# Four attention and feed-forward stages on one core: loads moved ahead, input normalised inside local attention, token shift started early, value projections of latent attention split

## The reference

```python
def _layer(x, wqkv, qs, ksc, wo, lg, lb, w1, b1, w2, b2):
    h = shift_token(x)                      # half of the features from the row before
    q, k, v = split(h @ wqkv)               # 8 heads of 64
    q, k = rotary_xpos(l2norm(q) * qs, l2norm(k) * ksc)
    x = x + local_attention(q, k, v) @ wo
    h = layernorm(shift_token(x)) * lg + lb
    a, g = split(h @ w1 + b1)
    return x + (a * gelu(g)) @ w2 + b2
```

## Time and profile before

| | us |
|---|---|
| median of 3 runs (4442.75 to 4448.69) | 4447.3 |
| the profiled execution | 4451.65 |
| its span, first to last instruction | 4449.6 |
| TensorE busy | 3951.2 |
| VectorE busy | 3057.0 |
| ScalarE busy | 2683.5 |
| GpSimd busy | 1837.7 |

### The profile page before, as it was taken

One profiled execution on the slowest core, in us unless ns is written; L12 is line 12 of the kernel. 1 busy time (PEld: TensorE's weight loads), 2 busy tenths in 40 slices (PEclk: granted clock), 3 DMA queues, 4 the chain that ended last, 5 costly groups with the idle time before them and its releaser, 6 DMA issues. The chain is left out here.

```text
span 4449.6 us, 104983 instructions
## 1 busy us (share of the span) xinstructions
PE 3951.2 (89%) x35227; PEld 3054.4 (69%) x35481; DVE 3057.0 (69%) x7210; ACT 2683.5 (60%) x6345; POOL 1837.7 (41%) x1769
## 2 busy tenths in 40 slices
PE   5999999938999988899999788999999999989999
PEld 4777777726666665566666546777767776669998
DVE  5888888867888865688888574555555555546666
ACT  4888888827777762477777325555555555533333
POOL 3555555446655541356565233333333333321111
PEclk9999999969999999999999899999999999999999
DMA  1000000010000001000000010000000000000000
GB/s 52 1 0 0 0 0 0 0 33 15 12 14 12 14 12 29 15 15 12 14 12 14 20 37 4 1 0 0 0 0 0 0 0 0 0 21 10 8 9 10
DMA packets 65662, 44.39 MB, mean 10 GB/s; under 512 B 39656, under 2 KB 54000, under 8 KB 65408
## 3 DMA queue, kind: packets, MB, share of 16 engines
q1 hardware_dynamic: 65568, 43.16, 3.9%
HBM read 13.53 MB, written 4.19 MB: 4 GB/s over the span
## 5 line engine op out<-in xcount | busy, mean ns | idle before, releaser
L1603 ACT ACTIVATE l_probs<-l_act,l_neg_max 128x128 f32<-128x128 f32 (+1 forms) x1024 | 415.9, 425 | 341.0 <-DVE l_neg_max L1560 338.7
L1544 POOL TENSOR_TENSOR l_probs<-l_probs,l_sums 128x512 f32<-128x512 f32 x384 | 391.5, 1041 | 452.6 <-DVE l_sums L1568 452.6
L1560 DVE TENSOR_REDUCE l_neg_max<-l_act 128x2 f32<-128x512 f32 (+1 forms) x384 | 247.0, 685 | 472.2 <-remote 193.7
L381 POOL TENSOR_TENSOR t_probs<-t_probs,t_neg_max 128x512 f32<-128x512 f32 x384 | 392.8, 1044 | 392.2 <-DVE t_neg_max L436 392.2
L429 DVE SCALAR_TENSOR_TENSOR t_probs<-t_tanh_qk,scalars_sb,t_dve 128x512 f32<-128x512 f32 x384 | 269.6, 743 | 88.3 <-ACT t_tanh_qk L532 38.2
L1920 ACT ACTIVATE e_hT<-e_act 128x512 f32<-128x512 f32 x256 | 153.0, 598 | 285.9 <-PE e_act L1939 285.9
L854 POOL TENSOR_TENSOR w_swappedQ<-w_rawQ,w_table 128x512 f32<-128x512 f32 x128 | 162.5, 1288 | 372.2 <-ACT w_rawQ L1032 361.1
L532 ACT ACTIVATE t_tanh_qk<-t_act,t_inv_beta 128x512 f32<-128x512 f32 x384 | 243.1, 684 | 91.7 <-PE t_act L597 91.3
L854 POOL TENSOR_TENSOR w_swappedK<-w_rawK,w_table 128x512 f32<-128x512 f32 x128 | 228.8, 1809 | 129.3 <-ACT w_rawK L1032 129.3
L1951 PEld LDWEIGHTS e_dve<-e_sb,e_hT 128*128 128x128 f32 x2048 | 269.4, 192 | 13.3
L1666 PE MATMUL l_dve<-ident_sb,l_probs 128*128 128x128 f32 x1536 | 211.3, 278 | 68.5 <-POOL l_probs L1544 67.6
(11 more groups left out here) (262 smaller groups left out, 10669.3 us busy)
## 6 DMA issues: line engine op xcount, KB each, us to landing
w_v_mid<-w_v SPq DMA_DIRECT2D x128, 130.0 KB, 2.3
m_h<-z SPq DMA_DIRECT2D x32, 128.0 KB
out<-x_sb SPq DMA_DIRECT2D x32, 128.0 KB, 1.8
m_h<-z SPq DMA_DIRECT2D x32, 127.0 KB
wqkv_sb<-L_ffn_wqkv SPq DMA_DIRECT2D x2, 768.0 KB, 6.0
m_h<-z SPq DMA_DIRECT2D x64, 0.2 KB
kv_up_sb<-L_attn_w_kv_up SPq DMA_DIRECT2D x1, 1024.0 KB, 4.9
e_sb<-L_ffn_w SPq DMA_DIRECT2D x1, 1024.0 KB, 5.4
```

Source lines behind the costliest of these rows:

```text
L381: nc.gpsimd.tensor_tensor(p, p, neg_max[:, j, 0:len(gs)].unsqueeze(2) .broadcast_to((P, len(gs), P * (t + 1))), ALU.add).then_inc(shifted. ...
L1544: nc.gpsimd.tensor_tensor(p, p, sums[:, at, 0:len(hs)].unsqueeze(2) .broadcast_to((P, len(hs), P * (t + 1))), ALU.mult).then_inc(divided.s ...
L1560: nc.vector.tensor_reduce(neg_max[:, units.index(name), 0:len(hs)], to_act.bank("s" + name, back)[:, :].rearrange("p (h j) -> p h j", h=le ...
L1603: ins = nc.scalar.activation(probs[:, at % SLOTS, s * width:(s + 1) * width], bank[:, s * width:(s + 1) * width], ACT.Exp, bias=neg_max[:, ...
```

## The change

- Loads become objects: `start` issues the DMAs, `wait` stands on an engine. The constants' block issues the first four sequences of x and the token weights and doesn't wait for them; token attention's block issues the rest of x and the ffn and latent weights; latent attention's block issues the expert weights. Engines wait where they first read. Constants that no stage reads are dropped.
- `normalise` is gone. In the first layer's local attention VectorE measures and scales the sequence ahead into `z_copy`, GpSimd takes the inverse root between its K and Q work, and SP stores `z_copy` to z.
- In local attention's step TensorE takes "zT" after scores 1, and "out" also waits until "zT" is drained; ScalarE takes the squares of Q ahead of the copies to `hT`, the raw copy of Q after them.
- The first two groups of token-shifted rows are fetched in local attention's block, after SP's last value move, and the two row-end copies of a group become one.
- In latent attention v0.0 and v1.0 are projected in turn 0 instead of 2; the first scores wait for k1, the fourth turn's for k3.

```diff
+    if entered:
+        entered()
     with eng.Fori(0, (n_seq - 4) // 2) as k:
...
 token_attention
+            @block.sync
+            def _(sp):
+                behind(sp)
             def _(dve):
+                c["token_loaded"].wait(dve)
+                c["x_first"].wait(dve)
...
-                pipeline(dve, n_seq, step, 4)
+                pipeline(dve, n_seq, step, 4, entered=lambda: c["x_rest"].wait(dve))
...
 window_attention, GpSimd
                 def step(ahead, front, back, done):
-                    for kind in "KQ" if front else "":
-                        sin(kind, front)
-                        power(kind, front)
+                    if front:
+                        sin("K", front)
+                        power("K", front)
+                    if ahead and first_layer:
+                        rsqrt(ahead)
+                    if front:
+                        sin("Q", front)
+                        power("Q", front)
 SP
+                    if ahead and first_layer:
+                        sp.wait_ge(copied.sem, copied.done("z", ahead))
+                        sp.dma_start(ahead.tiles(z), z_copy[:, :, :]).then_inc(stored, 16)
...
                 pipeline(sp, n_seq, step, 4)
+                short.wait_drained(sp, "out", Seq(2 * TILES - 1, 1, n_seq))
+                for number in range(2):
+                    shift.start(sp, z, Seq(number, number, n_seq // 2))
 VectorE
+                def input_moments(ahead):
+                    for t in range(TILES):
+                        ins = nc.vector.bn_stats(stats[:, t], ahead.tile(x, t))
+                    ins.then_inc(measured.sem, 1)
+                    wait_apart(nc, dve, c, measured.sem, measured.done("stats", ahead))
+                    for t in range(TILES):
+                        ins = nc.vector.bn_aggr(mv[:, t], stats[:, t])
+                    ins.then_inc(measured.sem, 1)
+                def input_scaled(ahead):
+                    input_free(ahead)
+                    if not ahead.first:
+                        dve.wait_ge(stored, 16 * ahead.number)
+                    dve.wait_ge(rst.sem, rst.done("rstd", ahead))
+                    for t in range(TILES):
+                        ins = nc.vector.tensor_scalar(z_copy[:, t], ahead.tile(x, t), mv[:, t, 0:1],
+                                                      rstd[:, t:t + 1], ALU.subtract, ALU.mult)
+                    ins.then_inc(copied.sem, 1)
...
                         cosines("K", front)
-                    if ahead:
+                    if ahead and first_layer:
+                        input_moments(ahead)
+                    elif ahead:
...
                             .then_inc(turn.sem, 1)
+                    if ahead and first_layer:
+                        input_scaled(ahead)
                     if back:
                         maxima(1, back)
...
                     if done:
+                        if first_layer:
+                            dve.wait_ge(stored, 16 * done.number + 16)
 ScalarE
                         y_taken(1, done)
+                    if front:
+                        squared_("Q", front)
                     if ahead:
                         short.wait_filled(act, "zT", ahead)
...
                     if front:
-                        squares_and_copy("Q", front)
+                        raw_taken("Q", front)
 TensorE
                         y_transposed(1, done)
+                    if back:
+                        scores(1, back)
                     if ahead:
                         pe.wait_ge(copied.sem, copied.done("z", ahead))
                         transposed("zT", ahead, [z_copy[:, t] for t in range(TILES)])
                     if back:
-                        scores(1, back)
                         probs_transposed(0, back)
                     if done:
                         short.wait_free(pe, "out", done)
+                        if ahead:
+                            short.wait_drained(pe, "zT", ahead)
                         short.wait_drained(pe, "yT1", done)
...
+class Shift:
+    def start(self, sp, z, seq):
+        h, done, half, whole = self.h[seq.parity], self.done[seq.parity], slice(D // 2, D), quad(seq, z)
+        ends = whole[P - 1:P, :, half].rearrange("p (s a) d -> p s a d", a=TILES)
+        heads = h[0:1, :, half].rearrange("p (s a) d -> p s a d", a=TILES)
+        sp.dma_start(h[:, :, 0:D // 2], whole[:, :, 0:D // 2]).then_inc(done, 16)
+        sp.dma_start(h[1:P, :, half], whole[0:P - 1, :, half]).then_inc(done, 16)
+        sp.dma_start(heads[:, :, 1, :], ends[:, :, 0, :]).then_inc(done, 16)
...
 gated_mlp, SP
-                    if ahead:
...
+                    if ahead and not (isinstance(ahead.number, int) and ahead.number < 2):
+                        sp.wait_ge(vec.sem, vec.done("xn", ahead.before().before()))
+                        shift.start(sp, z, ahead)
...
 ffn_layers
-        normalise(nc, n_seq, x, z, c)
...
 latent_attention
-    projected_at = {2: ["v0.0", "v1.0"], 3: ["v0.1", "v1.1"]}
+    projected_at = {0: ["v0.0", "v1.0"], 3: ["v0.1", "v1.1"]}
+    factors_at = {0: "k1", 3: "k3"}
...
-                    if job == "yT0":
-                        to_act.wait_drained(pe, "v1.1", back)
+                    if job in ("yT0", "yT2"):
+                        to_act.wait_drained(pe, {"yT0": "v1.0", "yT2": "v1.1"}[job], back)
...
-                    if back:
-                        to_act.wait_drained(pe, "k3", back)
                     for i in range(turns):
+                        if back and i in factors_at:
+                            to_act.wait_drained(pe, factors_at[i], back)
...
 build
+                def with_constants(sp):
+                    loads["x_first"].start(sp)
+                    loads["token_loaded"].start(sp)
+                def with_tokens(sp):
+                    loads["x_rest"].start(sp)
+                    loads["ffn_loaded"].start(sp)
+                    loads["latent_loaded"].start(sp)
+                set_constants(nc, c, d, with_constants)
+                token_attention(nc, n_seq, x, token_w, c, with_tokens)
...
+        latent_attention(nc, n_seq, x, latent_w, c, c["experts_loaded"].start)
```

More of the change, by code:

```diff
@@ L1357, in step @@
                         u = front.parity
[L1358 removed]
+                        wait_apart(nc, dve, c, shift.done[u], shift.total(front), 2)
                         moments("", front, [h[u][:, t] for t in range(QUAD)], stats, mv)
@@ L1993, in _, with __init__, start, wait @@
                 sp.wait_ge(finished, 16 * n_seq)
-def load(nc, name, pairs):
-    with nc.semaphore(name) as loaded, nc.Block() as block:
-        @block.sync
-        def _(sp):
-            for out, source in pairs:
-                sp.dma_start(out, source).then_inc(loaded, 16)
-            sp.wait_ge(loaded, 16 * len(pairs))
-def chip_constants(nc, ctx, d):
+class Load:
+    def __init__(self, nc, ctx, name, pairs):
+        self.sem, self.pairs = ctx.enter_context(nc.semaphore(name)), pairs
+    def start(self, sp):
+        for out, source in self.pairs:
+            sp.dma_start(out, source).then_inc(self.sem, 16)
+    def wait(self, eng):
+        eng.wait_ge(self.sem, 16 * len(self.pairs))
+def chip_constants(nc, ctx):
     def sb(name, shape, dt=F32):
         return ctx.enter_context(nc.sbuf_tensor(name, shape, dt))
-    c = {
+    return {
         "ident": sb("ident_sb", [P, P]),
@@ L2036, in chip_constants, with _ @@
+        ready = staging.enter_context(nc.semaphore("constants_ready"))
+        loaded = Load(nc, staging, "constants_loaded", [
+            (c["ident"][:, :], d["ident"]), (mask[:, :], d["mask"]), (window[:, :], d["window_mat"])])
         with nc.Block() as block:
+            @block.sync
+            def _(sp):
+                loaded.start(sp)
+                behind(sp)
             @block.vector
             def _(dve):
-                for out, source in ((c["ident_bf"], c["ident"][:, :]),
-                                    (c["mask_cols"], masks[:, 1]), (c["mask_window"], window[:, :]),
-                                    (c["pick"], pick[:, :]), (c["pick8"], pick8[:, :])):
+                nc.vector.memset(c["minus_half"][:, :], -0.5).then_inc(ready, 1)
+                nc.vector.memset(c["eps"][:, :], LN_EPS).then_inc(ready, 1)
+                loaded.wait(dve)
+                for out, source in ((c["ident_bf"], c["ident"][:, :]), (c["mask_window"], window[:, :])):
```

328 lines of the change are left out of this document (145 added, 183 removed).

## The result

The kernel after takes **4148.22 us** in the median of four runs (4146.71 to 4149.94), beside 4446.38 for the kernel before in the same comparison: a ratio of 0.9331, with a 95% interval of 0.9317 to 0.9344. The forecast was 4169 in a range of 4135 to 4232. In the five comparisons of this document the kernel before took between 4443.55 and 4448.69 us, so a difference of under some 5 us between kernels of different comparisons says nothing by itself; where one is that small, the traces decide.

A forecast was written before the change was run, and what follows sets the result against it. TensorE was nearly full in long stages, leaving empty stretches and its small stalls. 25 + 57.2 - 4 + 38 + 21.7 + 11.5 + 18.5 + 110 = 278 off 4451.65, less 4.35, gave 4169 us; range 4135 to 4232.

The forecast's parts named there:

- Start: Kernel start: token loads issued ahead of other loads, VectorE's first work at 9.5 instead of 34.45; 25 us off.
- The third rival: Kernel start: 9 MB of loads behind token attention's first steps hold up its code or weights; 4194 to 4214, chance 0.05.
- From token to local attention: Between these stages: ffn loads and separate normalisation leave the gap, first copy ready at 939.4 instead of 996.68; 57.2 us off.
- The charge of 4 for filling: First local attention's filling: second sequence's scaling stands behind unit keys and their power, raw queries behind transposed input; 4 us lost.
- The window step: Local attention's steady step: the 0.65 stall before transposing z goes, 0.7 us a step; 38 us off.
- The first rival: Local attention: the stall only moves, "out" waits as long for the drained z; 38 us more, 4207, chance 0.13.
- Scalings: First local attention layer: the scalings of the input take 0.60 each, other bound 1.1 more.
- the rival drawn from the Trainium skill's page: First local attention layer: GpSimd holds up VectorE's scalings, 1.1 in 31 steps; 4203, chance 0.05.
- Gated layers: Both gated layers: early fetch saves 21.7 us at the starts; one copy fewer shortens SP's cycle inside, 11.5 us.
- The one-engine rival: Gated layers: the one DMA engine carrying the long copy sets the cycle; 8.5 us more, 4178, chance 0.04.
- Latent attention: Latent attention: waits of 0.88 and 1.82 mostly go and the clock rises to 1.00; 110 us off.
- The second rival: Latent attention: clock stays low, or projections don't fit the hole; 32 to 50 us more, 4201 to 4219, chance 0.14.

The follow-up runs named there:

- experiment 3: Kernel after with the separate normalisation of all 64 tiles put back ahead of the first layer, loads still early: 4179.8 us.
- experiment 2: Kernel after with TensorE's and ScalarE's old order back in both local attention layers: 4216.29 us; with ScalarE's old order alone: 4147.61 us.
- the last version of experiment 5: Kernel after, local attention: yT0, V0 and V1 earlier on TensorE, first-layer inverse root and scaling earlier, squares of Q behind transposed input's copies: 4080.72 us.
- experiment 5: Kernel after, local attention: yT0 and V0 ahead of queries' transposes, 4134.28 us; also V1 ahead of scores 0, first-layer inverse root and scaling earlier, 4121.49 us.
- experiment 4: Kernel after, gated layers: two row-end copies, 4155.11 us; first two groups fetched in own block, 4167.54; copy of 127 partitions split into 112 and 15, 4147.56.
- experiment 1: Kernel after, latent attention: first scores wait for k3 again, 4176.62 us; or v0.0 and v1.0 projected in turn 2 again, 4232.4 us.
- moving two jobs ahead: Kernel after with yT0 and V0 ahead of the queries' transposes in local attention: 4134.28 us.
- a second edit: Added to the version with yT0 and V0 ahead: V1 projected ahead of scores 0, first-layer inverse root and input scaling earlier: 4121.49 us.
- the third in the same step: Added to the version with yT0, V0 and V1 earlier: ScalarE's squares of Q moved behind the copies of the transposed input: 4080.72 us.
- the changed gated layer: Kernel after, VectorE's order changed in the second gated layer: scaled rows ahead of the leaving group's statistics, that group's scaling last: 4182.59 us.
- an edit priced at 17: Kernel after with the row ends of a group copied by two DMAs again in the gated layers: 4155.11 us.

## Why the prediction was right

**Start.** 25 forecast, 26.1 measured. The first token load to the first work is 6.86 us (2.62 to 9.48), near the 6.07 plus half a microsecond. No wait for a load shows in token attention. The third rival fell.

**From token to local attention.** 57.2 forecast; the gap is 4.84 instead of 62.22, so 57.4. Its split is known by experiment 3. The charge of 4 for filling was mis-sized: from the first input copy to the first "out" the kernel before took 52.6 us and this one takes 57.8, which is 5.2, and beside the kernel of experiment 3, with the new order and no normalisation inside, it is 7.4. The mechanism is the one named.

**The window step.** The term that was most off, with latent attention's steps next. The forecast took 0.7 a step from start to start and 38 in all; it is 0.85, and 58 steady steps give 49. The two local attentions together brought 12 us more than forecast, in spite of the longer filling; steps and ends account for 26 us of the first and 25 of the second, where 19 each were forecast. The step that failed is the price of the stall: 0.65 is what the profile lists, and the records behind a wait are longer too. In experiment 2, 0.65 listed comes back as 0.85, and in the last version of experiment 5 a wait of 0.96 turned into 1.06. I had "out" start at 1308.1 instead of 1308.89; it starts 0.75 earlier, and the other 0.1 lies in the records around. The first rival didn't occur in this kernel, and experiment 5 shows how near it was: once TensorE no longer waited 0.81 ahead of scores 0, it did, with 0.69.

**Scalings.** 0.60 as taken, and no GpSimd work beside them, so the rival drawn from the Trainium skill's page "SBUF — State Buffer", section "Who interferes with whom", didn't come up. Something like it shows on the other side: GpSimd's inverse root takes 1.74 to 1.77 us behind the keys' power, beside VectorE's additions, and 0.70 where experiment 5 puts it ahead. That two engines held each other up there is my reading, not shown.

**Gated layers.** Starts: 10.85 forecast, 10.90 by the idle time (11.75 to 0.85). Inside: 11.5 forecast, 15.5 measured (22.0 + 15.3 - 21.8). I took 8.75 as TensorE's own group, namely 9.18 less the 0.41 that was listed; the sum that the prediction gives, 100 less 4.5 by eleven, makes 8.68. It is 8.36: again a listed wait stood for twice its size. In the second layer it is 8.79. VectorE has the leaving group's statistics there too, which I hadn't looked at; that this is the cause is not shown. The one-engine rival had the right mechanism (experiment 4) and the wrong price, since the blocked issue, not the transfer, closed the cycle, and with one copy less it closes in time.

**Latent attention.** 110 forecast, 115.8 by the trace (124.7 less 9.0 of the switch). The steady step is 36.09 against a forecast of 36.15, and the clock 1.00. From the second sequence's scores to the last one's, 30 steps came down from 39.80 to 36.09, which makes 111 where 108 was forecast. The stage's head up to there brought 3.5, where I took 2: waits of 0.69 and 2.04 for TensorE became none and 0.32. Its end brought 1.1, where I had nothing. The second rival fell, and experiment 1 shows that the falls of the clock here came with the wait of 1.82.

**The sum.** 302.1 in the span against 278: 12 in the windows, 6 in latent attention, 4 in the gated layers, 1 at the start and 1 at the two switches. Against that, the execution profiled before stood 4.35 above its median and this one 1.1, which takes 3 back. That is the 21.

## What to carry to other kernels

A listed wait of TensorE was a lower bound for the price of its stall in this kernel: where it went and no other took its place, 1.1 to 2 times what was listed came back, and more where the clock had fallen behind it. The wait of 1.82 us cost three times what the one of 0.88 did (84.2 against 28.4), over the same steps. When an engine is sped up, ask which wait comes next: moving two jobs ahead gave 14 us of a possible 50, a second edit 13, and only the third in the same step, one without effect by itself, the 41 that brought the whole to 67.5. Edits that look separate can need each other, as the normalisation inside the step needed the new order.

## What the runs showed that was not expected

- The clock fell for 3.4 us behind 22 of 27 equal waits of 1.82 us, never behind one of 0.87, and in the changed gated layer behind some pairs of 0.66 and 1.29.
- A DMA over 127 partitions held SP's queue, so that the next issue took 6.37 us; over 112 and 15 it took 0.69.
- A lead of two fetched groups hid a cycle that was 0.4 to 0.8 us too long for five to ten groups, so that an edit priced at 17 cost 7.
